# A two-layer transformer block on one core: third shared product in tiles of 128 tokens, four changes of order beside it

## The reference, cut to what matters

```python
# layer 0: one-head cross attention with a layernorm behind it, then a mixture of experts
x = x + layernorm(softmax(masked(q @ k.T / 16)) @ v @ Wo + bo) * g0 + beta0   # q from norm(x), k and v from ctx
h = norm(x)
weights, indices = top_k(softmax(h @ gate_w + gate_b), 2)
form = lambda h, w1, w2, w3: (silu(h @ w1 + b1) * (h @ w2 + b2)) @ w3 + b3
x = x + mean over 2 of form(h, sw1, sw2, sw3) + weighted sum over the 2 chosen of 8 of form(h, rw1, rw2, rw3)
# layer 1: cross attention with 16 heads of 16 (no mask), then a linear layer with a low-rank part
x = x + attention(norm(x) @ Wq.T, ctx @ Wk.T, ctx @ Wv.T) @ Wo.T
x = x + norm(x) @ (W + C @ V_r.T).T + b
```

## Time and profile before

| | us |
|---|---|
| median of three runs | 754.68 (752.0, 754.68, 754.7) |
| the profiled execution | 749.47 |
| its span, first to last instruction | 747.7 |
| PE busy | 727.4 |
| DVE busy | 462.2 |
| ACT busy | 311.0 |
| POOL busy | 271.7 |

### The profile page before, as it was taken

The page is one execution under the profiler, slowest core; times in us unless marked ns, Lnnn a source line. Parts: engine busy times, 40 slices in busy tenths (PEclk is TensorE's granted clock), DMA queues, the critical chain, the costliest instruction groups (busy, mean ns, idle before and its releaser), DMA issues.

```text
span 747.7 us, 15572 instructions
## 1 busy us (share of the span) xinstructions
PE 727.4 (97%) x5802; PEld 560.2 (75%) x5802; DVE 462.2 (62%) x1052; ACT 311.0 (42%) x556; POOL 271.7 (36%) x320
## 2 busy tenths in 40 slices
PE   8999999999999999999999999999998999999996
PEld 6776667666766575699999998989766667677774
DVE  4678663557355668534444655738677868788625
ACT  1323211422142121245555554644246755565571
POOL 5976225423410624402201515124734435205051
PEclk9999999999999999999999999999999999999998
DMA  9898944631521595722453423454887776755001
GB/s 263 224 301 265 203 117 154 187 122 41 180 71 52 188 374 171 250 59 82 118 143 88 126 76 95 121 143 133 244 223 193 183 184 175 199 140 127 28 3 50
DMA packets 73069, 113.87 MB, mean 152 GB/s; under 512 B 14930, under 2 KB 59347, under 8 KB 71075
## 3 DMA queue, kind: packets, MB, share of 16 engines
q1 hardware_dynamic: 60928, 80.17, 37.4%
q10 hardware_dynamic: 5906, 17.03, 8.4%
q0 software_dynamic: 6160, 15.67, 6.7%
HBM read 84.27 MB, written 28.41 MB: 151 GB/s over the span
## 4 chain that ended last, share of the span: by engine, by line
PE 87%; DVE 4%; POOL 2%; ACT 2%; issue 1%; DMA 1%; another core or an unknown queue 1%; ACTq 0%; SPq 0%; DVEq 0%; POOLq 0%
PE ps L1463 15%; PE ps L1092 12%; PE ps L1472 7%; PE ps L1109 7%; PE ps L2186 5%; PE ps L2215 5%; PE ps L1128 5%; PE ps L2206 4%; PE ps L1140 3%; PE ps L1062 3%; PE ps L1034 3%; PE ps L2179 2%; PE ps L2160 2%; DVE mxh L1836 2%; PE ps L1069 2%; PE ps L2115 2%
## 5 line engine op out<-in xcount | busy, mean ns | idle before, releaser
L1836 DVE TENSOR_REDUCE mxh<-ps 112x2 f32<-112x750 f32 x128 | 115.1, 932 | 34.2 <-PE ps L2186 31.3
L1463 PE MATMUL ps<-rowsT,w 128*128 128x128 f32 x1120 | 130.8, 275 | 0.0
L1463 PEld LDWEIGHTS ps<-rowsT,w 128*128 128x128 f32 x1120 | 128.0, 192 | 0.1
L2036 ACT ACTIVATE d_pT<-ps 125x448 f32<-125x448 f32 x192 | 92.0, 549 | 46.3 <-PE ps L2206 42.0
L1092 PE MATMUL ps<-x1T,sw 128*128 128x448 f32 x256 | 101.3, 540 | 0.0
L1417 ACT ACTIVATE w<-rw 128x1024 f32 x70 | 73.8, 1056 | 64.4 <-PE ps L1463 57.3
L1092 PEld LDWEIGHTS ps<-x1T,sw 128*128 128x128 f32 x256 | 47.6, 190 | 38.8 <-issue 35.9
L1356 POOL DMA_DIRECT2D yscr<-y x35 | 19.7, 563 | 153.8 <-DVE y L1390 153.8
L1472 PE MATMUL ps<-rw,h 128*128 x280 | 66.4, 380 | 0.0
L2186 PE MATMUL ps<-kst,qst 96*112 96x375 bf16 x256 | 58.4, 332 | 3.0 <-DVE mxh L1836 1.6
L902 ACT ACTIVATE silu<-ps,sb 128x448 f32<-128x448 f32 x32 | 20.3, 634 | 96.9 <-PE ps L1092 88.9
(11 more groups left out here) (259 smaller groups left out, 1193.3 us busy)
## 6 DMA issues: line engine op xcount, KB each, us to landing
kst<-kscr SPq DMA_DIRECT2D x39, 378.0 KB, 5.3
rw<-in_rw SPq DMA_DIRECT2D x24, 512.0 KB
kscr<-ka SPq DMA_DIRECT2D x16, 567.0 KB
cT<-in_ctx_t SPq DMA_DIRECT2D x17, 378.0 KB, 4.7
ctxT<-in_ctx_t SPq DMA_DIRECT2D x16, 378.0 KB
ctxn<-in_ctx SPq DMA_DIRECT2D x16, 336.0 KB
qst<-qscr ACTq DMA_DIRECT2D x12, 448.0 KB, 7.0
rows<-xg SPq DMA_DIRECT2D x35, 128.0 KB
```

The source lines that it names most:

```text
L1463: last = mm(bank[1 + 2 * q + k][:, block], w12[:, k, c, block], rowsT[:, q, c * P:(c + 1) * P], start=c == 0, stop=c == C - 1)
L1836: V.tensor_reduce(mxh[:, b % 2, 2 * g:2 * g + 2], ps[0:S, p:p + 2, 0:K], axis=AX_X, op=ALU.max).then_inc(s["s_max"], 1)
L2036: A(pT[:, q % 2, k, :], bank[4 + k][0:KC, 0:QUAD * S], ACT.Exp).then_inc(s["p_ready"], 1)
```

## The change

1. *Third shared product in tiles of 128 tokens.* `gluT` gets slots of 128 for its four sequences; `glu` writes 112 of each. Of an even group only sequences 0 to 2 have tiles of their own. The 112 tokens of its sequence 3 are put in the 16 free places of seven tiles: 48 by one copy, `deal`, into the three tiles of the same group, 64 by one copy, `carry`, into the four tiles of the next (odd) group. A tile gives 128 rows in PSUM: VectorE copies rows 96 to 127 to `extra` and adds the first 112 to `x_res` as before; ACT issues a DMA (`load_spread`) of the last 16 rows to their places in `spread`, and after seven tiles VectorE adds `spread` to `x_res` (`spread_out`, in the loop for i = 3 and beside the third routed tile). 14 tiles, numbered through `SHARED = (0, 3, 7, 10, 14)`. PE waits also for `dealt` in even groups and for `extra_ready` wherever it waits for `sh_read`. The orders of `keys`, `values` and `down` change around them for odd i.
2. `sw3` is loaded after the routing constants and the inputs of groups 2 and 3, behind a wait for `sw1` and `sw2`.
3. *Rows asked for ahead.* In the routed experts sync asks for the rows of tile n+1 before the biases of tile n.
4. *Values and queries on sync.* ACT's loads of values and queries inside the blocks are moved to sync, behind the maxima; the last group's results are issued by ACT.
5. *The last routing in pieces.* `tiles_counted`, `segments_begun` and `rows_of_tiles` are cut in two each and the pieces dealt out between the `glu` of group 3.

```diff
+EXTRA = P - S
+PAIR_TILES = GS * 2 // P
+SHARED = (0, G - 1, PAIR_TILES, PAIR_TILES + G - 1, 2 * PAIR_TILES)
...
+    def load_spread(eng, i, j):
+        d = SHARED[i] + j
+        eng.wait_ge(s["extra_ready"], d + 1)
+        if d == PAIR_TILES:
+            eng.wait_ge(s["glu_ready"], (i - 1) * U + U)
+        at = d % PAIR_TILES * EXTRA
+        eng.dma_start(spread[at:at + EXTRA, :], extra[S:P, d % 2, :]).then_inc(extra_out[d % 2], 16)
+    def extra_free(eng, d):
+        if d >= 2:
+            eng.wait_ge(extra_out[d % 2], 16 + d // 2 * 16)
...
+        def carry(i):
+            v.wait_ge(s["sh_ps"], SHARED[i])
+            V.tensor_copy(gluT[:].rearrange("p m (j t) -> p m j t", t=P)[:, :, :, S:P], dealt(G - 1, PAIR_TILES)).then_inc(done, 1)
+            n()
...
+        def deal(i):
+            v.wait_ge(s["glu_ready"], (i + 1) * U)
+            V.tensor_copy(gluT[:].rearrange("p m (j t) -> p m j t", t=P)[:, :, 0:G - 1, S:P], dealt(0, G - 1)).then_inc(s["dealt"], 1)
         def shared_out(i, j):
-            b = i * G + j
+            b, d = i * G + j, SHARED[i] + j
+            v.wait_ge(s["sh_ps"], d + 1)
+            extra_free(v, d)
+            V.tensor_copy(extra[P - 32:P, d % 2, :], bank[down_in(i, j)][P - 32:P, 0:D]).then_inc(s["extra_ready"], 1)
...
@@ vector, loop over i
             glu(i - 1, 7)
+            if i % 2:
+                deal(i - 1)
...
+                if i % 2:
+                    keys(b + 1)
+                    shared_out(i - 1, 0)
+                    shared_out(i - 1, 1)
+                    keys(b + 2)
+                    shared_out(i - 1, 2)
+                    carry(i)
@@ vector, group 3
         shared_out(i - 1, 2)
-        shared_out(i - 1, 3)
+        carry(i)
         rows_behind()
+        tiles_begun()
+        glu(i, 0, carried)
         tiles_counted()
-        glu(i, 0)
-        keys(15)
+        keys_read(15)
         glu(i, 1)
+        keys_parted(15)
         segments_begun()
+        glu(i, 2)
+        segments_summed()
         experts_of_tiles()
-        glu(i, 2)
+        glu(i, 3)
         rows_of_tiles()
-        glu(i, 3)
+        rows_summed()
+        glu(i, 4)
...
@@ tensor
-                last = mm(bank[down_in(i, j)][0:S, 0:D], gluT[:, m, j * S:(j + 1) * S], sw3[:, e, h, :], start=m == 0, stop=m == U - 1)
+                last = mm(bank[down_in(i, j)][:, 0:D], gluT[:, m, j * P:(j + 1) * P], sw3[:, e, h, :], start=m == 0, stop=m == U - 1)
...
-                down(i - 1, 1)
-                values(b + 1)
-                down(i - 1, 2)
+                if i % 2:
+                    values(b + 1)
+                    down(i - 1, 1)
+                else:
...
         positions(i)
-        down(i - 1, 3)
         up(i, 0)
@@ routed experts, sync
+        load_rows(0)
+        for n in range(NTILE):
+            q = n % 2
+            if n + 1 < NTILE:
+                load_rows(n + 1)
             e = sp.value_load(expert_row[0:1, n:n + 1], min_val=0, max_val=E - 1)
@@ layer 1, sync
                 maxima(b + 1)
+            if b and b + 1 < NV:
+                sp.wait_ge(s["pv_ps"], b)
+                load_values(b + 1)
+            if b in (G, 2 * G):
+                sp.wait_ge(s["st_ps"], b * 4 * NKC)
+                load_queries(sp, b // G + 1)
             what, i = blocks_in(b)
-            if what == "f":
-                results(i)
+            if what == "f" and i < NG - 2:
+                results_out(sp, i)
...
-        results(NG - 1)
+        results_out(sp, NG - 2)
@@ layer 1, scalar
-                if b + 1 < NV:
-                    load_values(b + 1)
             exps(b, 0)
             exps(b, 1)
-            if b in (G, 2 * G):
-                load_queries(a, b // G + 1)
...
         last_turned(5)
+        results_out(a, NG - 1)
```

More of the change, by code:

```diff
@@ L88, in first_layer @@
     cb = sb("cb", [S, 1])
-    bo_row = sb("bo_row", [1, D])
+    extra = sb("extra", [P, 2, D])
+    bo_row = extra[0:1, 1, :]
     bo_b = sb("bo_b", [S, D])
@@ L111, in first_layer @@
     silu = sb("silu", [P, 2, GS])
+    spread = rep[:].rearrange("p k c t -> p (k c t)")[0:S, 0:D]
     iota = sb("iota", [S, E])
@@ L509, in hidden_normalized, with dealt @@
             normalized("h", i, lambda j: xh_moe[:, i * G + j, :], s["xh1_ready"])
-        def glu(i, m):
-            v.wait_ge(s["silu_ready"], i * U + (m + 1))
[L513 to L517, removed]
+        def dealt(first, last):
+            at = (G - 1) * P
+            return gluT[:, :, at + first * EXTRA:at + last * EXTRA].rearrange("p m (j t) -> p m j t", t=EXTRA)
@@ L772, in _ @@
             output_stat(b)
+            if i == NG - 1:
+                spread_out(0)
             if i == 1:
                 keys_read(b)
-            glu(i - 1, 0)
+            glu(i - 1, 0, n.now() if i == 1 else carried)
             u_out(b + 1)
@@ L817, in _ @@
                 input_normalized(i + 1)
[L818 to L822, removed]
-                shared_out(i - 1, 3)
+                if i % 2:
[5 more added lines that the diff above has]
+                    carry(i)
+                    carried = n.now()
+                else:
+                    shared_out(i - 1, 0)
+                    keys(b + 1)
+                    shared_out(i - 1, 1)
+                    shared_out(i - 1, 2)
+                    keys(b + 2)
+                    shared_out(i - 1, 3)
                 offsets(i + 1)
@@ L993, in _, with beside @@
             silus(NG - 1, m)
-        experts["scalar"](a, second["scalar_beside"])
+        load_spread(a, NG - 1, 0)
+        load_spread(a, NG - 1, 1)
+        def beside(a, m):
+            if m == 1:
+                load_spread(a, NG - 1, 2)
+                load_spread(a, NG - 1, 3)
+            second["scalar_beside"](a, m)
+        experts["scalar"](a, beside)
         second["scalar"](a)
@@ L1182, in _ @@
             mm(bank[2][0:S, D:2 * D], rep[:, 1, k, :], wo[:, k, :], start=k == 0, stop=False)
-        mm(bank[2][0:S, D:2 * D], ones[0:1, 0:S], bo_row[:], start=False, stop=True).then_inc(s["fold_ps"], 1)
+        mm(bank[2][0:S, D:2 * D], ones[0:1, 0:S], bo_row, start=False, stop=True).then_inc(s["fold_ps"], 1)
         p_T(0)
@@ L1264, in _ @@
                 inputs_over(i + 1)
-                down(i - 1, 3, range(U // 2))
+                behind = shared_tiles(i - 1) - 1
+                down(i - 1, behind, range(U // 2))
                 if b + 2 < NV:
                     values(b + 2)
-                down(i - 1, 3, range(U // 2, U))
+                down(i - 1, behind, range(U // 2, U))
                 if b + 3 < NV:
@@ L1303, in _ @@
         t.wait_ge(s["rw_in"], 3 * 16 * E)
-        experts["tensor"](t, second["tensor_beside"], lambda: t.wait_ge(s["sh_read"], B))
+        experts["tensor"](t, second["tensor_beside"], lambda: t.wait_ge(s["sh_read"], SHARED[NG]))
         second["tensor"](t)
@@ L1335, in load_last_bias, with load_rows @@
             sp.dma_start(rb3[:, n % 2, :], dram["rb3"][bass.ds(e, 1), :].to_broadcast([P, D])).then_inc(s[f"rb3_in{n % 2}"], 16)
-        behind = None
-        for n in range(NTILE):
-            q = n % 2
+        def load_rows(n):
             at = sp.value_load(row_base[0:1, n:n + 1], min_val=0, max_val=ROWS - P)
@@ L1646, in since, with results_out @@
         return [(i, m - DONE[i]) for i in range(EARLY)]
+    def results_out(eng, i):
+        for j in range(G):
+            eng.wait_ge(s["res_ready"], i * G + (j + 1))
+            eng.dma_start(out[i * G + j], x_res[:, i * G + j, :]).then_inc(s["res_out"], 16)
     def sync(sp):
@@ L1658, in maxima @@
                 sp.dma_start(qst[i % 2][DEPTH + k:DEPTH + k + 1, :, j * S:(j + 1) * S], mT[k * NH:(k + 1) * NH, b % 2, :]).then_inc(s[f"mrow_in{b % 2}"], 16)
-        def results(i):
-            for j in range(G):
-                sp.wait_ge(s["res_ready"], i * G + (j + 1))
-                sp.dma_start(out[i * G + j], x_res[:, i * G + j, :]).then_inc(s["res_out"], 16)
         sp.wait_ge(routed["w2_ready"], NTILE)
```

101 lines of the change are left out of this document (73 added, 28 removed).

## The result

The changed kernel takes **742.38 us** (median of four, 741.4 to 743.03) against 753.76 (median of four, 752.0 to 754.7): ratio 0.986, 95% interval 0.9844 to 0.9877, 11.4 us less. The forecast was 745.4, inside its range but 3.0 too high; 0.9 of that is its base, since it took 9.3 off 754.68 and the median beside the changed kernel is 753.76. The profiled execution took 743.03 us, 6.4 less than that of before. The pair of profiles thus shows little more than half of the gain, and the first question is which of the two numbers the parts add up to.

A forecast was written before the change was run, and what follows sets the result against it. PE was taken as the bound, busy 727.4 of 747.7 us. Product 5.9, rows 1.6, queries 1.5 and end 0.3 sum to 9.3 off the median 754.7, giving 745.4 us; range 740.5 to 751.

The forecast's parts named there:

- Tiles at 3.45 each: Third shared product: 14 tiles of 128 tokens for 16 of 112, wider side free, two tiles gone, 6.9 us of PE.
- Tile of group 0: First third shared product: the added VectorE copy and the later values(5) are covered, so the dropped tile gains its full 3.45.
- Tile of group 2: Before group 3's up products: VectorE's work becomes as long as PE's, costing some 0.2, between 0 and 1.
- Experts' start: Start of the routed experts: scatters drain beside a full weight load, 0.6 us lost, between 0 and 2.5.
- rival (a): Experts' start starves: rows land 2.5 late, routing takes 1.0; gain 6.6, 748.1 us; chance 0.10.
- Dealing copy beside rstd: Group 2's dealing copy on VectorE falls beside GpSimd's rstd: 0.2 us charged, at most 0.7.
- Rows ahead: Routed experts: rows requested before the biases come a tile period sooner, both PE waits go, 1.6 us, 0.6 to 2.0.
- Queries: Attention blocks 4 and 8: query requests moved off ACT remove PE waits, 1.25 + 0.3 = 1.5 us, 0.5 to 2.8.
- Values: Attention blocks: values requested on sync behind the maxima land in 3.2 us, with 2.5 to spare; cost 0.
- (b): Values keep the median landing of 8.1, 2.4 late; five blocks lose 12, net 2.7 slower, 757.4 us; chance 0.10.
- (c): Values take the longest landing, 9.3, 3.6 late; five blocks lose 18, net 8.7 slower, 763.4 us; chance 0.06.
- End: Kernel's end: four of the last eight result requests go to ACT, gaining 0.3 us, at most 0.6.

The follow-up runs named there:

- no_rows_ahead: Changed kernel with sync asking for a tile's rows behind the last biases again: 745.72 us, ratio 0.9917 to the kernel before.
- routing_whole: Changed kernel with the last routing uncut, in the order of before, between the gated products of group 3: 744.62 us, ratio 0.99.
- before_rows: Kernel before with only the asking for rows ahead of the biases added: 750.14 us, ratio 0.9957.
- loads_on_act: Changed kernel with the loads of both queries and values in the attention blocks issued by ACT again: 745.12 us, ratio 0.9901.
- queries_on_act: Changed kernel with only the query loads of blocks 4 and 8 on ACT again: 743.79 us, ratio 0.9878.

## Why the prediction was right

The range held the result and the mechanisms were the ones forecast, with the end as the exception. The gain of 9.3 was too small, and its errors cancel in part: the product and the rows were taken too small, the queries and the end too large.

*Tiles at 3.45 each, 6.9 in all*: right; 48 records still take 10.36 us, and A to B fell by 7.05.

*Tile of group 0, 3.45*: half right. PE's start is behind the 0.36 copy as forecast. What I did not look for is keys(7) farther on. ACT reads them 1.6 to 1.7 us after PE has ended them in four of the nine profiles of the new product, 1.0 after in four, and 0.2 in no_rows_ahead. In the first four PE waits 0.54 to 0.61 for VectorE, and A to B is 0.7 longer. ACT's program waits there for PE and for the store of keys(5), which had the same buffer; that store was issued at 113.50 and the DMA share was 0.05 from 120 to 124 us, so it had long left. What coincides is GpSimd's issue of the scatters of group 0. In the kernel before the last of the eight was over at 128.0 and PE ended these keys at 133.2; now the last starts at 131.26, and in the eight late profiles ACT reads 0.4 or 1.0 to 1.1 us behind that start (in no_rows_ahead ahead of it). That the scatters hold ACT up is not shown; no run tested it.

*Tile of group 2, cost 0.2*: right with a small error on the safe side, the cost is 0. The mechanism, that the pieces let this tile count, is shown by routing_whole. The first glu came at 283.62 and not at my 285.1, because I had left out, for VectorE and for PE alike, that the tile of group 0 moves this stage by 3.45: 285.1 - 3.45, plus 1.24 for the later A of this profile and 0.75 for the keys' wait, is 283.6.

*Experts' start, 0.6*, and rival (a): nothing was lost. DMA is full until 308 in the changed kernel (until 310 before) and the rows were asked for at 311.01, only 2.2 before they were used instead of 3.4; the lead that was there absorbed it.

*Dealing copy beside rstd, 0.2*: the two rstd steps took 0.41 and 1.72 where they took 0.92 and 1.04, 0.17 more, and PE's idle is 0.20 against 0.16. The step that is long, 0.92 before and 1.72 after, is the one beside VectorE's last subtraction of the keys (0.94, at 261.58 and at 260.24), and not beside a cast as I had read it. The Trainium skill ("SBUF — State Buffer", on the shared port pair) was not put to the test: the copy ended at 259.74 and GpSimd's first step began at 259.88.

*Rows ahead, 1.6 (0.6 to 2.0)*: this is **the step that failed**. The runs show 3.0 to 3.3, above my upper bound of 2.0. The mechanism was right; the size was read from one execution that lay below all others of its kernel. I had said so in the first paragraph, and corrected only the sum's base for it, not the terms, though a wait for a DMA is just what differs between executions. The two later profiles of that kernel show the waits that this one lacked, 2.5 and 2.6 us for 1.2.

*Queries, 1.5 (0.5 to 2.8)*: 1.3 in block 8, and nothing in block 4, where PE waits 0.60 for VectorE's maxima in both kernels (598.48 before, 593.33 after). Of the 0.3 that I added for block 4 nothing came.

*Values, 0*, and rivals (b) and (c): right. The landing was estimated at 3.2 and is 3.2 to 8.8, median 4.0; PE waited for values nowhere. The Trainium skill ("DMA: Bandwidth & Descriptors", Queues, rings and completion order), from which rival (b) took that the values lose their turn behind the keys on one row, did not decide: the values' requests at 574.65, 584.01 and 592.73 came 8.3, 7.0 and 6.3 us behind the block's first request for keys, and the DMA share around them was 0.08, 0.29 and 0.22, so most of the keys had landed.

*End, 0.3*: wrong; it is 0, since the span ended 5.7 us behind VectorE's last result with the last requests on one queue or on two. *Rival (d)*: VectorE does pace group 3 in the uncut order alone.

In sum, for an ordinary execution: 6.3 to 7.05 for the product, 3.3 for the rows, 1.3 for the queries, 0 for the end, 10.9 to 11.6; measured 11.4 and 9.8, and 10.1 by the ratios of the halves. The first pair of profiles shows 6.4 because its before was a quick execution: by the stretches -1.24 (A) + 6.24 + 0.72 + 0.72 = 6.4. In it the third product has lost 0.8 to the keys' wait, the rows were worth only 0.7 up to C, and a fall of the clock, which its before did not have, took 1.1 from the last stretch.

## What to carry to other kernels

Compare the profiled execution with the median before sizing anything: if it is quicker, the waits that vary, those for DMAs above all, are under-represented in it, and their terms need a wider upper bound than its rows give. When a product is made shorter, VectorE work that stood between others has to be cut finer by as much, or the saving ends as a wait one stage later. A request that waits for nothing should not stand in a queue behind one that waits for an engine.

## What was not expected of the hardware

A pause of all compute engines: at 554.8 and 565.9 us (561.4 and 572.3 in the kernel before) PE stands 0.96 and 1.5 us, and ACT and VectorE take up what PE had ended up to 1.6 us before. It is in twelve of the fourteen profiles in this form. It begins 0.4 to 0.7 us behind the start of a gather of GpSimd (553.42 and 563.65), though two other pairs of gathers bring none; ACT's late reads of the keys at 132 us likewise come while GpSimd issues indirect DMAs. Whether these are one thing no run tested. Behind the longer pause the granted clock fell to 0.50, from 2.4 to 1.2 GHz, for some 3 us in six of the twelve, and the idle ahead does not separate them: 1.50 to 1.58 us with a fall and 1.43 to 1.57 without. In before_rows it fell at 555.5, behind shorter waits.

A pause of 0.7 to 1.4 us within a run of equal products, where nothing in the program waits, in three profiles (loads_on_act, queries_on_act, before_rows), all of kernels in which ACT issues the queries' loads. But the three profiles of the kernel before lack it, and in before_rows it stands ahead of the requests of block 4, so the reason stays open.
